# Two transformer layers on one core: small VectorE and GpSimd jobs handed to ScalarE, GpSimd and TensorE

## The chip, the core and the metric

The kernel runs on one core of a Trainium2 chip. The metric is device time in microseconds, the median of several executions; lower is better. A core has TensorE (PE), VectorE (DVE), ScalarE (ACT), GpSimd (POOL) and SyncE (SP), which here only issues DMAs. Each engine works through its own list of instructions in order, and waits on semaphores for the others.

## The reference

The input x is 16 sequences of 256 tokens and 128 numbers. Two parts follow one another, each with a residual and a layer norm behind it:

```python
x = _layernorm(x + _L0_attn_ref(x, ...))      # gated convolution, then 16-head attention in chunks
x = _layernorm(x + _L0_ffn_ref(x, ...))       # two layers of the kind below
def _layer(x, wqkv, qs, ksc, wo, lg, lb, w1, b1, w2, b2):
    h = shift_token(x)                         # half of the columns come from the token before
    q, k, v = split(h @ wqkv)                  # 8 heads of 64
    q, k = l2norm(q) * qs, l2norm(k) * ksc     # l2norm divides by max(norm, 1e-12)
    q, k = rotary_xpos(q, k)
    o = local_attention(q, k, v)               # windows of 64 queries, 128 keys, softmax
    x = x + o @ wo
    h = layernorm(shift_token(x)) * lg + lb
    a, g = split(h @ w1 + b1)                  # 341 + 341 columns
    return x + (a * gelu(g)) @ w2 + b2
```

All is float32. The change touches only the two layers of the second part.

## The kernel before

The kernel has two stages. Stage A does the first part for all 16 sequences; it is not touched. The second stage ("the layers") takes 16 sequences through layer 0 and then layer 1, so 32 units of work. A unit has two tiles of 128 tokens, and each engine's list runs in steps of one tile: an even step (tile 0) and an odd step (tile 1), 64 in all. A loop iteration holds four steps (two units). Nothing is scheduled by a program: the order in which the work of several units is interleaved is written out by hand in each engine's `body`.

A step works on several units at once. For the unit at hand it does the scores, the softmax and the values. For the next unit it prepares q, k and v. For units before it does what follows attention, with lags counted in steps in `F_LATE` ("stats" 4, "norm" 5, "residual" 5, "mT" and "gates" 6, "values" and "down" 7, "yo" 8, "z" 9). So a job with an even lag is done in even steps, and one with an odd lag in odd steps.

The names that matter, by engine, in the order of a step:

- TensorE: the scores (L1420 the mask, L1427 q times k); in an even step the transpose `mT` of the normed hidden state; q or k of the next unit (L1354); the transposes of the softmax weights (L1440); the output product (L1465); q or k again (L1354); a transpose of normalised q or k (L1359); weights times values (L1454); another L1359; v (L1354); in even steps the hidden products (L1372), in odd steps the last product `down` (L1392), which waits for `uT`.
- VectorE: maximum of the scores `fmx` (L1182) and their difference from it (L1186); even steps `hT2 = mT * ln_g + ln_b` (`scaled`, L1085) and `yo` (L1115), odd steps `uT` (L1092) and the layer norm `hc` (`normalised`, L1077, two instructions); the rotation of q or k (L1052, L1053) and its sum of squares (L1055); `mid` (L1146); the sum of the exponentials `f_sum` (L1165) and its reciprocal `f_rsum` (L1168); in odd steps the other two `uT`; the second rotation; and the guard of the norms (`guard`, L1063), which is max(norm squared, 1e-24) on 128x16.
- GpSimd: the multiplication of q or k by the inverse norms (`normalise`, L662, a pair); the sum of the rotated halves (`sums`, L646); the division of the softmax weights by their sums, that is 128x1024 times a broadcast `f_rsum` (L720); in even steps `mrstd` (L688, L690); `sums` again; the inverse norms by a power of -1/2 (`inverse_norms`, L654); in odd steps the residual (`residual`, L698, which adds the second bias b2 to `mid`, and for layer 1 also L704, which adds the residual of stage A).
- ScalarE: squares (L811), copies out of the matmul banks (L873, L832, L886, L823), the exponentials (L878), and in even steps three gelus (L858). A change from exponentials to gelus and back loads a table.

Of the kernel before, what the change touches and what calls it, by code (L numbers as in the profile page):

```python
# [169 lines left out]
def build(nc, t):  # L170

    ctx = ExitStack()
    with ctx:
# [73 lines left out]
        def in_queries(p, at):  # L247
# [34 lines left out]
        resb = [sb(f"resb{p}", [P, 2, TILES, DIM]) for p in range(PAIR)]  # L282
# [150 lines left out]
        def layer_weights(l):  # L433
# [4 lines left out]
            yield b2[l][:, :], t["b2"][l].partition_broadcast(P)  # L438
# [152 lines left out]
        def _(pool):  # L591
            pool.memset(ones[:, :], 1.0).then_inc(consts_set, 1)
            pool.memset(halves[:, :], -0.5).then_inc(consts_set, 1)
            pool.memset(eps[:, :], LN_EPS).then_inc(consts_set, 1)
# [974 lines left out]
```

## Time and profile before

| | |
|---|---|
| median of 3 runs | 1438.56 us (1438.05 to 1438.8) |
| the profiled execution: its own time | 1443.03 us |
| its span, first to last instruction | 1441.2 us |
| stage A | from the start to about 700 us |
| the layers | from about 700 us to the end |
| granted TensorE clock, mean | 0.971 of full speed |

The profile is of one execution. Spans of rows are from the start of the span. A row's duration contains the tail of an instruction, so on VectorE the next one begins some 0.08 us before the end of the one before.

### The profile page before, as it was taken

The page shows a single profiled execution, that of the slowest core. Times are in us where ns is not written, and L with a number is a line of the kernel's source. Part 1 is how long each engine was busy: PE and PEld are TensorE (multiplying, and loading weights), DVE is VectorE, ACT ScalarE, POOL GpSimd, SP SyncE. Part 2 cuts the span into 40 slices and gives each one's busy share as a digit, 9 for nine tenths or more (in the row PEclk, how much of TensorE's full clock was granted, in tenths as well). Part 3 has the DMA queues.
Part 4 walks back from the last instruction along what each step waited for, and adds up shares of the span by engine and source line. Part 5 has one row for each costly group of instructions (what it writes and reads, how often), then busy time and mean ns, then how long its engine had stood idle before and what let it go on. Part 6 is the DMA issues. An engine that isn't in the chain of part 4 may idle for free.

```text
span 1441.2 us, 35736 instructions
## 1 busy us (share of the span) xinstructions
PE 1266.9 (88%) x12288; PEld 987.5 (69%) x12288; DVE 1294.1 (90%) x2514; ACT 872.1 (61%) x1468; POOL 951.0 (66%) x753
## 2 busy tenths in 40 slices
PE   5889899989989889988788999999999889999986
PEld 3577677767767767766566777777777767777764
DVE  4899999999999999997798988999899898999975
ACT  3556566565666656554456676676676657666661
POOL 0733443344433444346799899999999999999973
PEclk8899999999999999998899999999999999999998
DMA  5000000000000000000111112111111121212111
GB/s 170 1 10 13 12 5 11 11 11 11 9 11 11 11 7 5 8 9 14 36 44 41 41 41 49 38 39 42 45 45 48 41 50 43 51 40 49 45 30 31
DMA packets 87332, 44.24 MB, mean 31 GB/s; under 512 B 43938, under 2 KB 80460, under 8 KB 87244
## 3 DMA queue, kind: packets, MB, share of 16 engines
q1 hardware_dynamic: 87244, 43.08, 12.0%
q8 instruction: 54, 0.88, 0.3%
q14 instruction: 34, 0.28, 0.1%
HBM read 19.99 MB, written 6.29 MB: 18 GB/s over the span
## 4 chain that ended last, share of the span: by engine, by line
DVE 39%; issue 23%; POOL 19%; PE 15%; SPq 2%; DVEq 1%; ACT 1%; POOLq 1%; DMA 0%; ACTq 0%
DVE sums L973 9%; DVE probs L1005 7%; POOL rnorm L654 5%; DVE mx L999 4%; POOL kT L646 4%; POOL kT L662 4%; POOL probs L720 4%; PE bank L1372 3%; DVE xo L1034 2%; PE bank L1359 2%; PE bank L1454 2%; PE bank L1427 2%; DVE hc L1077 2%; SPq L475 1%; DVE conv L916 1%
## 5 line engine op out<-in xcount | busy, mean ns | idle before, releaser
L622 POOL TENSOR_TENSOR probs<-probs,coef 128x1024 f32<-128x1024 f32 x128 | 239.5, 1901 | 202.3 <-DVE coef L965 202.3
L795 ACT ACTIVATE probs<-probs 128x1024 f32<-128x1024 f32 x128 | 134.8, 1053 | 100.5 <-DVE probs L1005 100.0
L654 POOL TENSOR_TENSOR rnorm<-norm,halves 128x16 f32<-128x16 f32 x64 | 187.4, 2928 | 3.3
L1274 PE MATMUL bank<-ident,probs 128*128 128x128 f32 x1024 | 143.4, 285 | 49.6 <-POOL probs L622 49.6
L999 DVE TENSOR_REDUCE mx<-bank 128x8 f32<-128x512 f32 x256 | 163.8, 681 | 16.5 <-PE bank L1287 15.2
L782 ACT ACTIVATE wT<-bank 128x512 f32<-128x512 f32 x256 | 138.9, 596 | 65.4 <-PE bank L1274 64.4
L646 POOL TENSOR_TENSOR kT<-qT 128x512 f32<-128x512 f32 x128 | 162.9, 1273 | 22.5 <-DVE qT L1053 20.0
L1005 DVE TENSOR_TENSOR probs<-bank,mx 128x512 f32<-128x512 f32 x256 | 163.6, 680 | 0.0
L1274 PEld LDWEIGHTS bank<-ident,probs 128*128 128x128 f32 x1024 | 115.9, 145 | 68.6 <-POOL probs L622 57.5
L1287 PE MATMUL bank<-kT,qT 64*128 64x256 f32 x1024 | 155.7, 425 | 5.4 <-DVE probs L1005 5.4
L811 ACT ACTIVATE qT<-bank 128x512 f32<-128x512 f32 x128 | 75.9, 593 | 134.0 <-PE bank L1354 126.4
L1313 PE MATMUL bank<-wT,v 128*64 128x128 f32 x2048 | 145.8, 286 | 11.4 <-DVE gate L911 5.7
L973 DVE TENSOR_REDUCE sums<-probs 128x16 f32<-128x1024 f32 x128 | 153.2, 1208 | 0.0
L1313 PEld LDWEIGHTS bank<-wT,v 128*64 128x64 f32 x2048 | 114.4, 141 | 50.3 <-issue 22.0
L720 POOL TENSOR_TENSOR probs<-probs,f_rsum 128x1024 f32<-128x1024 f32 x64 | 121.4, 1897 | 36.0 <-DVE f_rsum L1168 36.0
L662 POOL TENSOR_TENSOR kT<-kT,rnorm 128x512 f32<-128x512 f32 x128 | 131.4, 1047 | 2.7
L1182 DVE TENSOR_REDUCE fmx<-bank 128x4 f32<-128x512 f32 x128 | 82.5, 686 | 51.1 <-PE bank L1427 49.9
L1359 PE MATMUL bank<-ident,kT 128*128 128x128 f32 x512 | 82.7, 285 | 46.2 <-POOL kT L662 44.8
L1287 PEld LDWEIGHTS bank<-kT,qT 64*128 64x128 f32 x1024 | 93.8, 198 | 36.4 <-issue 22.6
L1359 PEld LDWEIGHTS bank<-ident,kT 128*128 128x128 f32 x512 | 57.2, 143 | 77.8 <-POOL kT L662 40.4
L633 POOL TENSOR_TENSOR rstd<-mv,eps 128x1 f32<-128x1 f32 x32 | 6.2, 192 | 157.3 <-DVE mv L1028 157.3
L1372 PE MATMUL bank<-hT,w 128*128 128x256 f32 (+1 forms) x384 | 96.9, 388 | 11.4 <-DVE mid L1146 9.3
(118 smaller groups left out, 3074.2 us busy)
## 6 DMA issues: line engine op xcount, KB each, us to landing
probs<-f_v SPq DMA_DIRECT2D x96, 128.0 KB, 2.3
res<-stage_x SPq DMA_DIRECT2D x48, 128.0 KB, 3.7
xn<-in_x SPq DMA_DIRECT2D x16, 128.0 KB, 2.2
xr<-in_x SPq DMA_DIRECT2D x16, 128.0 KB, 2.1
stage_x<-xo SPq DMA_DIRECT2D x32, 64.0 KB, 1.6
hn<-stage_x SPq DMA_DIRECT2D x32, 64.0 KB
mn<-mid SPq DMA_DIRECT2D x64, 32.0 KB
stage_x<-yo SPq DMA_DIRECT2D x16, 128.0 KB, 2.1
```

The costliest lines, as they stand in the source:

```text
L622: nc.gpsimd.tensor_tensor(out=e[:, :, :, :], in0=e[:, :, :, :], in1=coef[r][:, 2, A_REP * ng:A_REP * (ng + 1), :].unsqueeze(3).broadcast_t ...
L646: nc.gpsimd.tensor_tensor(out=qk[m][:, :, :], in0=on_self[m % 2][:, :, :], in1=on_partner[m % 2][:, :, :], op=ALU.add).then_inc(added, 1)
L654: nc.gpsimd.tensor_tensor(out=rnorm[:, at], in0=norm2[:, 1, at], in1=halves[:, 0:2 * F_HEADS], op=ALU.pow).then_inc(rnorm_set, 1)
L662: nc.gpsimd.tensor_tensor(out=qk[m][:, :, :], in0=qk[m][:, :, :], in1=rnorm[:, F_HEADS * m:F_HEADS * (m + 1)].unsqueeze(2).broadcast_to([P ...
L720: nc.gpsimd.tensor_tensor(out=e, in0=e, in1=f_rsum[s % 2][:, :, :].unsqueeze(3).broadcast_to([P, 2, 4, F_KEYS]), op=ALU.mult).then_inc(f_n ...
L973: nc.vector.tensor_reduce(sums[at % 2][:, A_REP * gg:A_REP * (gg + 1), :], E[(s - SUM_LAG) % E_RING][:, :, :, :], AX.X, ALU.add).then_inc( ...
L999: ins = nc.vector.tensor_reduce(m[:, 2 * k:2 * k + 2, :], both[k][:, :].rearrange("p (h c k) -> p h c k", h=2, c=CHUNKS), AX.X, ALU.max)
L1005: ins = nc.vector.tensor_tensor(e[:, 2 * k:2 * k + 2, :, :], both[k][:, :].rearrange("p (h c k) -> p h c k", h=2, c=CHUNKS), m[:, 2 * k:2 ...
L1274: ins = nc.tensor.transpose(banks[4 + hp][:, P * (2 * kb + hh):P * (2 * kb + hh + 1)], e[:, 2 * hh + hp, 2 * kb:2 * kb + 2, :], ident[:, :])
L1287: ins = nc.tensor.matmul(banks[2 * (s % 2) + h % 2][:, SEQ * (h // 2):SEQ * (h // 2 + 1)], qT[p][lo:lo + A_HD, 2 * g + h // 2, P * tile:P ...
L1313: ins = nc.tensor.matmul(bank[A_HD * hh:A_HD * (hh + 1), P * hp:P * (hp + 1)], v[ap][:, kb, A_HD * og:A_HD * (og + 1)], wT[hp][:, kb, hh, ...
L1359: ins = nc.tensor.transpose(bank[:, P * block_of:P * (block_of + 1)], flat[:, P * block_of:P * (block_of + 1)], ident[:, :])
```

## The change

Five jobs of the layers go to another engine, and the arithmetic stays the same.

1. The division of the softmax weights: GpSimd divides five of eight heads (128x640 instead of 128x1024), and ScalarE the other three, with three copies of 128x128 that are scaled by a column of `f_rsum` (`divided`). TensorE's transposes of the weights wait for both.
2. The guard of the norms goes from VectorE to GpSimd, into `inverse_norms` ahead of the power.
3. The second bias b2 becomes row 85 of the last piece of w2, and row 85 of that piece of `uT` is set to 1 once, at the start. So the last matmul of `down` has 86 rows instead of 85, and no add of b2 is left.
4. The residual: in layer 0 it is now a copy of `mid` on ScalarE (`kept`); in layer 1 it is one add on GpSimd (`mid` and `res1`) where there were two.
5. `hT2 = mT * ln_g + ln_b` goes from VectorE to ScalarE (`hidden_input`), at the start of an even step.

```diff
+F_NORM_ACT = 3
+NORM_FLOOR = 1e-24
@@ weights
-            yield b2[l][:, :], t["b2"][l].partition_broadcast(P)
+            yield w2[l][F_ROWS[-1]:F_ROWS[-1] + 1, F_CHUNKS - 1, :], t["b2"][l:l + 1, :]
@@ gpsimd, start
+            for p in range(PAIR):
+                pool.memset(uT[p][:, F_CHUNKS - 1, :], 1.0).then_inc(consts_set, 1)
@@ gpsimd, inverse_norms
+                    pool.wait_ge(consts_set, N_CONSTS)
+                    pool.wait_ge(norm_step, 4 * unit + 2 * tile + 2)
+                    nc.gpsimd.tensor_scalar_max(norm2[:, 1, at], norm2[:, 0, at], NORM_FLOOR).then_inc(guarded, 1)
                     pool.wait_ge(guarded, TILES * unit + tile + 1)
@@ gpsimd, residual
-                    nc.gpsimd.tensor_tensor(out=resb[p][:, 0, :, :], in0=mid[p][:, :, :],
-                                            in1=b2[layer][:, :].unsqueeze(1).broadcast_to([P, TILES, DIM]),
-                                            op=ALU.add).then_inc(mid_read, 1)
-                    if layer == LAYERS - 1:
-                        pool.wait_ge(res1_in[p], 16 * (it + local // PAIR + 1 - TURNS * layer))
-                        pool.wait_ge(mid_read, unit + 1)
-                        nc.gpsimd.tensor_tensor(out=resb[p][:, 1, :, :], in0=resb[p][:, 0, :, :], in1=res1[p][:, :, :],
-                                                op=ALU.add).then_inc(resb_set, 1)
+                    pool.wait_ge(res1_in[p], 16 * (it + local // PAIR + 1 - TURNS * layer))
+                    nc.gpsimd.tensor_tensor(out=resb[p][:, :, :], in0=mid[p][:, :, :], in1=res1[p][:, :, :],
+                                            op=ALU.add).then_inc(resb_set, 1)
@@ gpsimd, body (residual is called for layer 1 alone)
-                            e = fE[s % F_RING]
+                            e = fE[s % F_RING].rearrange("p k a n -> p (k a) n")[:, 0:F_HEADS - F_NORM_ACT, :]
+                            inverse = f_rsum[s % 2][:, :, :].rearrange("p k a -> p (k a)")[:, 0:F_HEADS - F_NORM_ACT]
                             pool.wait_ge(f_rsum_set, n + 1)
@@ scalar
+                def hidden_input(it, local, layer):
+                    unit = PAIR * it + local
+                    act.wait_ge(f_made["mT"], unit + 1)
+                    nc.scalar.activation(hT2[local % PAIR][:, :], f_bank("mT", local, "middle")[:, 0:SEQ], ACT.Identity,
+                                         bias=ln_b[layer][:, 0:1], scale=ln_g[layer][:, 0:1]).then_inc(f_read["mT"], 1)
+                def kept(it, local):
+                    p, unit = local % PAIR, PAIR * it + local
+                    act.wait_ge(f_read["out"], TILES * unit + TILES)
+                    wait(act, f_read["down"], unit - 1)
+                    nc.scalar.activation(resb[p][:, :, :], mid[p][:, :, :], ACT.Copy).then_inc(mid_kept, 1)
+                def divided(n, s):
+                    e = fE[s % F_RING]
+                    act.wait_ge(f_rsum_set, n + 1)
+                    for a in range(4 - F_NORM_ACT, 4):
+                        ins = nc.scalar.activation(e[:, 1, a, :], e[:, 1, a, :], ACT.Copy, scale=f_rsum[s % 2][:, 1, a:a + 1])
+                    ins.then_inc(f_divided, 1)
@@ scalar, body, behind values_read
+                        if f_exists(turn, s):
+                            divided(n, s)
+                        local = f_late(turn, s, "residual")
+                        if local is not None and layer_of(local) < LAYERS - 1:
+                            kept(it, local)
@@ vector
-                def guard(index, unit, tile):
-                def scaled(it, local, layer):
@@ tensor
+                                rows += c == F_CHUNKS - 1
                     pe.wait_ge(f_normed, late + 1)
+                    pe.wait_ge(f_divided, late + 1)
```

GpSimd, from the division of an odd step in layer 0 to the second `sums` of the even step behind it. Before:

```order
L720 TENSOR_TENSOR probs<-probs,f_rsum 128x1024
L646 TENSOR_TENSOR kT<-qT 128x512
L654 TENSOR_TENSOR rnorm<-norm,halves 128x16
L698 TENSOR_TENSOR resb<-mid,b_0 128x256
L662 TENSOR_TENSOR kT<-kT,rnorm 128x512 x2
L646 TENSOR_TENSOR kT<-qT 128x512
L720 TENSOR_TENSOR probs<-probs,f_rsum 128x1024
L688 TENSOR_TENSOR mrstd<-mmv,eps 128x2
L690 TENSOR_TENSOR mrstd<-mrstd,halves 128x2
L646 TENSOR_TENSOR kT<-qT 128x512
```

The same place in the changed kernel:

```order
L721 TENSOR_TENSOR probs<-probs,f_rsum 128x640
L649 TENSOR_TENSOR kT<-qT 128x512
L657 TENSOR_SCALAR norm<-norm 128x16
L660 TENSOR_TENSOR rnorm<-norm,halves 128x16
L668 TENSOR_TENSOR kT<-kT,rnorm 128x512 x2
L649 TENSOR_TENSOR kT<-qT 128x512
L721 TENSOR_TENSOR probs<-probs,f_rsum 128x640
L694 TENSOR_TENSOR mrstd<-mmv,eps 128x2
L696 TENSOR_TENSOR mrstd<-mrstd,halves 128x2
L649 TENSOR_TENSOR kT<-qT 128x512
```

The division is smaller, a guard stands ahead of each power, and nothing stands any more between the power of an odd step and the pair of multiplications that opens the even step.

ScalarE, from the copy of v in an even step to the second half of the next odd step's weights (wq holds the transposed weights). Before:

```order
L823 ACTIVATE f_v<-bank 128x512
L858 ACT_TABLE_LOAD
L858 ACTIVATE ge<-bank,b_0 128x256 x2
L858 ACTIVATE ge<-bank,b_0 85x256
L816 ACTIVATE fhT_high<-bank 128x256
L811 ACTIVATE qT<-bank 128x512
L873 ACTIVATE wq<-bank 128x512 x2
L878 ACT_TABLE_LOAD
L878 ACTIVATE probs<-probs 128x1024
```

The same place in the changed kernel:

```order
L824 ACTIVATE f_v<-bank 128x512
L881 ACTIVATE probs<-probs,f_rsum 128x128 x3
L859 ACT_TABLE_LOAD
L859 ACTIVATE ge<-bank,b_0 128x256 x2
L859 ACTIVATE ge<-bank,b_0 85x256
L817 ACTIVATE fhT_high<-bank 128x256
L812 ACTIVATE qT<-bank 128x512
L899 ACTIVATE wq<-bank 128x512 x2
L904 ACT_TABLE_LOAD
L904 ACTIVATE probs<-probs 128x1024
```

The three scaled copies stand ahead of the gelus, and so also ahead of the next step's exponentials; the number of table loads is the same.

## Rows read from the trace of the kernel before

**Rows 1.** The page: busy time, share of the span, instructions of each engine.

```profile
PE 1266.9 (88%) x12288; PEld 987.5 (69%) x12288; DVE 1294.1 (90%) x2514; ACT 872.1 (61%) x1468; POOL 951.0 (66%) x753
```

**Rows 2.** Busy time by stretch: PE, PEld, DVE, ACT, POOL, clock, DMA share, GB/s.

```profile
900.00:1000.00 100.00, 93.39 (x1019) 72.84 (x1018) 91.34 (x180) 66.37 (x106) 90.33 (x67) 1.00 0.17 39
1250.00:1350.00 100.00, 89.69 (x983) 70.33 (x976) 91.42 (x202) 64.57 (x104) 94.97 (x78) 1.00 0.19 46
```

**Rows 3.** Timeline, VectorE, one unit in layer 0: start, duration, line, count, idle before.

```profile
907.83 0.68 DVE L1053 TENSOR_TENSOR qT<-bank,table 128x512 f32<-128x512 f32 x1
...
910.51 1.29 DVE L1182 TENSOR_REDUCE fmx<-bank 128x4 f32<-128x512 f32 x2 [0.62 <-PE bank L1427]
...
912.91 0.54 DVE L1085 TENSOR_SCALAR hT<-bank,ln_g,ln_b 128x256 f32<-128x256 f32 x1
...
916.92 0.20 DVE L1168 RECIPROCAL f_rsum<-f_sum 128x8 f32<-128x8 f32 x1
...
920.91 1.29 DVE L1182 TENSOR_REDUCE fmx<-bank 128x4 f32<-128x512 f32 x2 [0.84 <-PE bank L1427]
...
924.04 1.32 DVE L1077 TENSOR_SCALAR hc<-mn,mmv,mrstd 128x128 f32<-128x128 f32 x2
...
927.27 1.20 DVE L1165 TENSOR_REDUCE f_sum<-probs 128x8 f32<-128x1024 f32 x1
...
932.73 1.29 DVE L1182 TENSOR_REDUCE fmx<-bank 128x4 f32<-128x512 f32 x2 [0.62 <-PE bank L1427]
```

**Rows 4.** Timeline, GpSimd, the same unit.

```profile
908.59 1.27 POOL L646 TENSOR_TENSOR kT<-qT 128x512 f32<-128x512 f32 x1
909.97 2.90 POOL L654 TENSOR_TENSOR rnorm<-norm,halves 128x16 f32<-128x16 f32 x1
912.83 0.73 POOL L698 TENSOR_TENSOR resb<-mid,b 128x256 f32<-128x256 f32 x1
913.52 2.05 POOL L662 TENSOR_TENSOR kT<-kT,rnorm 128x512 f32<-128x512 f32 x2
...
917.21 1.90 POOL L720 TENSOR_TENSOR probs<-probs,f_rsum 128x1024 f32<-128x1024 f32 x1 [0.41 <-DVE f_rsum L1168]
919.06 0.19 POOL L688 TENSOR_TENSOR mrstd<-mmv,eps 128x2 f32<-128x2 f32 x1
...
924.22 2.06 POOL L662 TENSOR_TENSOR kT<-kT,rnorm 128x512 f32<-128x512 f32 x2
```

**Rows 5.** Timeline, ScalarE, the same unit.

```profile
918.39 1.28 ACT L858 ACT_TABLE_LOAD   x1
...
924.84 1.06 ACT L878 ACTIVATE probs<-probs 128x1024 f32<-128x1024 f32 x1
```

**Rows 6.** Timeline, GpSimd and VectorE, the first odd step with `hc` beside loaded lists.

```profile
767.96 2.05 POOL L662 TENSOR_TENSOR kT<-kT,rnorm 128x512 f32<-128x512 f32 x2
...
768.28 1.81 DVE L1077 TENSOR_SCALAR hc<-mn,mmv,mrstd 128x128 f32<-128x128 f32 x2
```

**Rows 7.** Timeline, GpSimd, one unit in layer 1.

```profile
1281.05 1.90 POOL L720 TENSOR_TENSOR probs<-probs,f_rsum 128x1024 f32<-128x1024 f32 x1 [0.51 <-DVE f_rsum L1168]
...
1288.11 2.15 POOL L662 TENSOR_TENSOR kT<-kT,rnorm 128x512 f32<-128x512 f32 x2
...
1298.67 0.72 POOL L698 TENSOR_TENSOR resb<-mid,b 128x256 f32<-128x256 f32 x1
...
1300.24 2.04 POOL L662 TENSOR_TENSOR kT<-kT,rnorm 128x512 f32<-128x512 f32 x2
...
1304.03 1.90 POOL L720 TENSOR_TENSOR probs<-probs,f_rsum 128x1024 f32<-128x1024 f32 x1 [0.51 <-DVE f_rsum L1168]
```

**Rows 8.** Timeline, VectorE, the same unit in layer 1.

```profile
1287.77 0.59 DVE L1077 TENSOR_SCALAR hc<-mn,mmv,mrstd 128x128 f32<-128x128 f32 x2
...
1296.31 1.29 DVE L1182 TENSOR_REDUCE fmx<-bank 128x4 f32<-128x512 f32 x2
```

**Rows 9.** Costliest groups, whole run: busy us, mean ns, idle before.

```profile
L816 ACT ACTIVATE fhT_high<-bank 128x256 fp32r<-128x256 f32 x32 | 12.3, 385 | 13.5 <-PE bank L1346 13.5
```

More of the change, by code:

```diff
@@ L281, in build @@
         res1 = [sb(f"res1_{p}", [P, TILES, DIM]) for p in range(PAIR)]
-        resb = [sb(f"resb{p}", [P, 2, TILES, DIM]) for p in range(PAIR)]
+        resb = [sb(f"resb{p}", [P, TILES, DIM]) for p in range(PAIR)]
         yo = [sb(f"yo{p}", [P, TILES, DIM]) for p in range(PAIR)]
@@ L728, in body @@
                         local = f_late(turn, s, "residual")
-                        if local is not None:
-                            residual(it, local, layer_of(local))
+                        if local is not None and layer_of(local) == LAYERS - 1:
+                            residual(it, local, LAYERS - 1)
                 both_layers(pool, body, pre)
@@ L1039, in layers_program, with rotate @@
             def layers_program():
-                def rotate(index, local, m, turn, layer):
+                def rotate(index, before, local, m, turn, layer):
                     tile, kind = divmod(m, 2)
@@ L1079, in normalised @@
                     ins.then_inc(hc_set, 1)
-                def scaled(it, local, layer):
-                    unit = PAIR * it + local
-                    dve.wait_ge(f_made["mT"], unit + 1)
-                    nc.vector.tensor_scalar(hT2[local % PAIR][:, :], f_bank("mT", local, "middle")[:, 0:SEQ], ln_g[layer][:, 0:1],
-                                            ln_b[layer][:, 0:1], ALU.mult, ALU.add).then_inc(f_read["mT"], 1)
                 def gated_product(c, bank, col, par, unit, layer):
@@ L1112, in finished @@
                     dve.wait_ge(f_made["down"], unit + 1)
[L1113 removed]
+                    dve.wait_ge(resb_set if last_layer else mid_kept, b + 1)
                     wait(dve, m_out[par], 16 * (it + turn_of))
                     nc.vector.tensor_tensor(yo[par][:, :, :], f_bank("down", local, "middle")[:, 0:TILES * DIM].rearrange("p (t d) -> p t d", t=TILES),
[L1116 removed]
+                                            resb[par][:, :, :], ALU.add).then_inc(f_read["down"], 1)
                     if last_layer:
@@ L1143, in attended @@
                     dve.wait_ge(res_in[local % PAIR], 16 * (it + local // PAIR + 1))
-                    wait(dve, mid_read, unit - 1)
+                    if layer_of(local - PAIR) == LAYERS - 1:
+                        wait(dve, resb_set, unit - 1 - BATCH * (LAYERS - 1))
+                    else:
+                        wait(dve, mid_kept, unit - 1)
                     wait(dve, mn_in[local % PAIR], 80 * (it + local // PAIR))
@@ L1167, in exponentials_summed @@
                     wait(dve, f_normed, n - 1)
+                    wait(dve, f_divided, n - 1)
                     nc.vector.reciprocal(f_rsum[s % 2][:, :, :], f_sum[s % 2][:, :, :]).then_inc(f_rsum_set, 1)
@@ L1213, in body @@
                             at = 2 * tile + 1
-                            rotate(4 * (unit + 1) + at, 4 * (p + 1) + at, at, turn, layer_of(p + 1))
-                            guard(4 * (unit + 1) + at, unit + 1, tile)
+                            rotate(4 * (unit + 1) + at, unit, 4 * (p + 1) + at, at, turn, layer_of(p + 1))
                         if late("z") is not None and layer_of(late("z")) == LAYERS - 1:
```

38 lines of the change are left out of this document (15 added, 23 removed).

## The prediction

> **What bounds the kernel now.** I first read the busy shares [rows 1]. Over the whole span VectorE is at 90% and GpSimd at 66%, but GpSimd's share is an average of two stages. So I read the stretches of the layers [rows 2]: there GpSimd is at 90% in layer 0 and 95% in layer 1, VectorE at 91% in both, TensorE at 93% and 90%, ScalarE at 65%. Nobody is full; three engines hand work round in a ring and each waits a little. So no busy sum gives the time, and I followed the ring through one unit in the timeline.
>
> In layer 0 the even step's first maximum starts at 910.51 and the next unit's at 932.73 [rows 3]: a unit takes 22.22 us. The reader should see four links in it, of which I use the starts:
>
> - 910.51 to 917.21, 6.70 us: VectorE works from the maximum to `f_rsum` without a wait (it ends at 916.92 + 0.20), then GpSimd, which waited 0.41 us for it, starts the division [rows 3, 4].
> - 917.21 to 924.22, 7.01 us: GpSimd without a wait: division, `mrstd`, sum, power, up to the next step's pair of multiplications L662 [rows 4].
> - 924.22 to 925.36, 1.14 us: VectorE's pair `hc` starts at 924.04, and ends 1.32 us later [rows 3]. The same pair takes 0.59 us in layer 1, at 1287.77 [rows 8], where GpSimd's pair starts 0.34 us later than it [rows 7]. Here it starts 0.18 us later, and `hc` ends 0.1 us after the first of the two multiplications (2.06 / 2, so 925.25) [rows 4]. In an earlier unit L662 began first, at 767.96; `hc` came at 768.28, took 1.81 us and ended at 770.09, that is 0.08 us after the end of both multiplications [rows 6]. So one `hc` instruction that meets a running multiplication waits for its end. How many of the two are caught depends on a few tenths: none at a lead of 0.34 us, one at 0.18, both at a lag.
> - 925.36 to 932.73, 7.37 us: VectorE to `uT`, the last product on TensorE and the next scores [rows 3].
>
> 6.70 + 7.01 + 1.14 + 7.37 = 22.22: this ring sets layer 0. The Trainium skill, SBUF — State Buffer, section "Who interferes with whom", gives the reason: VectorE's two-port instructions and GpSimd's share a port pair as an exclusive lock, and whichever starts first makes the other wait for its whole instruction. The three cases above agree. Were the pair shared by bandwidth instead, `hc` would take about 0.6 us wherever it falls, the unit of layer 0 in the sum below would be 6.25 + 6.67 + 0.19 + 0.59 + 7.37 = 21.07 instead of 22.42, and the change would gain some 17 us there instead of losing 3.
>
> In layer 1 the unit is 1281.05 to 1304.03, 22.98 us [rows 7]. Its links are 7.72 (maximum at 1296.31 to division at 1304.03 [rows 7, 8]), 7.06 (1281.05 to 1288.11), and 8.20 from that pair to the next maximum (1288.11 to 1296.31), through TensorE alone, since `hc` is free there: 22.98.
>
> **The change, priced.**
>
> *Division.* GpSimd's broadcast multiplication takes 1.90 us for 1024 columns and 2.05 / 2 = 1.03 for 512 [rows 4]; on the line between them 640 columns take 1.25. That is -0.64 us (1.90 - 1.25, rounded) on the second link.
>
> *Guard on GpSimd.* A GpSimd instruction of this kind isn't in the trace. Below, the add of 128x2 takes 0.19 us [rows 4]; above, the power of the same 128x16 takes 2.90 [rows 4]. It is a plain elementwise operation like the first, and 14 more columns at the broadcast multiplication's 1.7 ns each (0.87 us for 512 columns) add 0.02; with a wait on its own result I take 0.30, between the two ends. On the second link: +0.30. On VectorE the guard's going saves a few tenths at the end of steps, where VectorE then waits for TensorE (0.62 and 0.84 us [rows 3]), so nothing.
>
> *`hT2` to ScalarE.* It takes 0.54 us on VectorE, of which 0.45 is start to start (the overlap is 0.08), in the first link [rows 3]: -0.45. On ScalarE 256 columns take 0.385 [rows 9] in a gap at the start of the even step.
>
> *Residual.* It lies between GpSimd's power and the pair of the even step: 912.83 to 913.52, in layer 1 1298.67 to 1300.24 [rows 4, 7]. It isn't in the ring above, but moves the pair of the even step, by which TensorE's scores and so `hc` are timed. Without it in layer 0 that pair could start 0.08 us behind the power's end at 912.87, so 0.57 earlier; in layer 1 one add is left, 1.57 - 0.73 = 0.84 earlier. The guard delays it: from the sum's start at 908.59 to the power's at 909.97 are 1.38 us now [rows 4], and will be 1.23 (the sum) + 0.30: +0.15. The shorter division gives nothing here, since that sum waits for the rotation, 907.83 + 0.68 = 908.51 [rows 3, 4].
>
> *ScalarE.* Three copies of 128 columns, each at least half of 0.385 us and at most all of it [rows 9], so 0.6 to 1.15 us a step; I take 0.8. In an even step they stand ahead of a table load that now starts as soon as it can, at 918.39, and push back all behind it. The next exponentials start at 924.84 and end at 925.90, and the sum that reads them starts at 927.27 [rows 3, 5]: 1.37 us of cover. So nothing; without the cover each tenth over it would cost a tenth per unit. The wait of TensorE for `f_divided` is covered by more than 2 us (the transposes come in the next step).
>
> *`down` with 86 rows, the two memsets, one DMA less broadcast:* nothing; the columns stream as before, and the start waits for DMAs.
>
> **Sum for layer 0.** New links: 6.70 - 0.45 = 6.25; 7.01 - 0.64 + 0.30 = 6.67. Where does `hc` fall? From the maximum, L662 starts at 6.25 + 6.67 = 12.92. `hc` starts behind three pieces: the even pair at 913.52 - 910.51 = 3.01, less 0.57, plus 0.15, so 2.59; to the odd maximum 7.39 (913.52 to 920.91); to `hc` 3.13 (920.91 to 924.04) [rows 3, 4]. Together 13.11, so it now lags by 0.19 us where it led by 0.18. Both of the pair are caught, as at 768.28, and it ends 2.13 us (770.09 - 767.96) after the start of L662 instead of 1.14. The unit: 6.25 + 6.67 + 2.13 + 7.37 = 22.42, that is 0.20 slower than now.
>
> **Sum for layer 1.** 7.72 - 0.45 = 7.27; 7.06 - 0.34 = 6.72; L662 at 13.99. `hc`: 3.93 (1296.31 to 1300.24) - 0.84 + 0.15 = 3.24, + 7.39 + 3.13 = 13.76. It leads by 0.23 us (now 0.34): one is caught. Then 7.27 + 6.72 + 1.14 + 7.37 = 22.50, against 22.98: -0.48. Through TensorE it would be 7.27 + 6.72 + 8.20 = 22.19, which no longer binds.
>
> **All.** The pattern of layer 0 holds from the fourth unit until the residual of layer 1 begins, some 15.5 units; that of layer 1 for some 11.6. 15.5 x 0.20 = +3.1; 11.6 x -0.48 = -5.6. In the first three units GpSimd has fewer jobs around it and, I estimate, its saving of 2 x 0.34 counts whole: -2. The last units and the tail: an estimate of -1.5 from one shorter division and less waiting. Sum -6.0. The profiled execution took 1443.03 us, 4.5 over the median; so 1437.0 for such a one and 1432.6 for the median.
>
> **The rivals.**
>
> - *The lag isn't reached in layer 0* (my phases are off by 0.3 us). One of `hc` is caught as now, and the other chain binds, through the even pair: it is 0.42 us earlier (0.57 - 0.15), 22.22 - 0.42 = 21.80. 15.5 x -0.42 = -6.5 instead of +3.1: 1423. For it: the phase is a difference of long chains. Against: it must err by 0.3 in one direction. 16%.
> - *In layer 1 none is caught* (a lead over 0.3): 22.19 a unit, -9.2 instead of -5.6: 1429. 10%.
> - *The other side: the guard on GpSimd costs more.* It is once on the ring of each of 27 units, so each 0.1 us costs 2.7 us. From 0.30 + 6.0 / 27 = 0.52 on, the change is no gain. At 0.7 it is +4.8: 1443. The far end, the power's 2.90 and a wait, would give 1432.6 + 27 x 2.7, about 1505; against it speaks that a power is no plain operation, and that the plain one of few columns takes 0.19 [rows 4]. 13%.
> - *Both are caught in layer 1* (a lead under 0.1): 23.5 a unit, +5.9 instead of -5.6: 1444. 10%.
> - *ScalarE becomes late* (copies with a scale from a column at over 1.37 us for three, or its waits): each step's exponentials hold VectorE. At 2 us, 0.6 x 32 = +19, less 6: 1452. 5%.
>
> The main forecast keeps 46%. **What follows.** A measurement of this kernel can tell about 0.2%, 2.9 us, from no change. Faster: 39 of the main case's 46 and both first rivals, 65%. Same: 12%. Slower: 23%. The range takes in the first rival and both of the slower ones near 1443: 1420 to 1443.
>
> **What would show it.** Right: L721 at 1.25 us, L657 near 0.2, units of 22.4 us in layer 0 with an `hc` pair of about 2 us, and of 22.5 in layer 1 with a pair of about 1.3. Waits of VectorE for the scores grow beyond 0.6 and 0.8 us. Wrong: `hc` pairs of 1.3 in layer 0; a guard over 0.5 us; `f_sum` waiting for ScalarE.

## The result, and the profile after

| | us, median (lowest to highest) |
|---|---|
| before, measured with it | 1438.68 (1438.05 to 1440.41), 4 runs |
| after | 1430.21 (1429.87 to 1431.28), 4 runs |
| ratio | 0.9939, 95% interval 0.9926 to 0.9951 |

The change makes the kernel 8.5 us faster. The profiled execution took 1430.35 us, with a span of 1428.5. The first part of the page of the kernel after, with the columns of [rows 1]:

```profile
PE 1258.4 (88%) x12288; PEld 984.8 (69%) x12288; DVE 1262.2 (88%) x2418; ACT 943.0 (66%) x1708; POOL 905.3 (63%) x787
```

Two stretches of it, for [rows 2] (length, busy time of each engine with the number of instructions, granted clock, DMA share, GB/s):

```profile
900.00:1000.00 100.00, 90.73 (x1001) 71.76 (x998) 86.77 (x164) 74.70 (x142) 82.11 (x70) 1.00 0.17 40
...
1250.00:1350.00 100.00, 91.77 (x1013) 72.33 (x1013) 90.53 (x194) 78.48 (x142) 91.25 (x87) 1.00 0.19 45
```

GpSimd fell from 90 to 82 in layer 0, and VectorE from 91 to 87. Yet layer 0 became slower, as the starts of the first maxima show. The timeline of VectorE after, for [rows 3] (start, duration, engine, line, operation, tiles, shapes, count, idle time before it and what ended it):

```profile
907.18 1.29 DVE L1202 TENSOR_REDUCE fmx<-bank 128x4 f32<-128x512 f32 x2 [1.41 <-PE bank L1445]
...
913.14 0.20 DVE L1188 RECIPROCAL f_rsum<-f_sum 128x8 f32<-128x8 f32 x1
...
917.32 1.29 DVE L1202 TENSOR_REDUCE fmx<-bank 128x4 f32<-128x512 f32 x2 [1.33 <-PE bank L1445]
...
920.44 1.94 DVE L1102 TENSOR_SCALAR hc<-mn,mmv,mrstd 128x128 f32<-128x128 f32 x2
...
929.75 1.29 DVE L1202 TENSOR_REDUCE fmx<-bank 128x4 f32<-128x512 f32 x2 [1.40 <-PE bank L1445]
```

And GpSimd in the same unit, for [rows 4]:

```profile
906.49 0.26 POOL L657 TENSOR_SCALAR norm<-norm 128x16 f32<-128x16 f32 x1
906.83 2.93 POOL L660 TENSOR_TENSOR rnorm<-norm,halves 128x16 f32<-128x16 f32 x1
909.93 2.04 POOL L668 TENSOR_TENSOR kT<-kT,rnorm 128x512 f32<-128x512 f32 x2 [0.17 <-POOL rnorm L660]
...
913.42 1.26 POOL L721 TENSOR_TENSOR probs<-probs,f_rsum 128x640 f32<-128x640 f32 x1 [0.21 <-DVE f_rsum L1188]
...
915.59 1.27 POOL L649 TENSOR_TENSOR kT<-qT 128x512 f32<-128x512 f32 x1
916.83 0.25 POOL L657 TENSOR_SCALAR norm<-norm 128x16 f32<-128x16 f32 x1
917.24 2.93 POOL L660 TENSOR_TENSOR rnorm<-norm,halves 128x16 f32<-128x16 f32 x1 [0.16 <-POOL norm L657]
920.25 2.05 POOL L668 TENSOR_TENSOR kT<-kT,rnorm 128x512 f32<-128x512 f32 x2
```

The unit is 907.18 to 929.75, 22.57 us (22.48 to 22.49 in every other one), against 22.22 before. Its links are 6.24 (907.18 to 913.42), 6.83 (to 920.25), 2.13 (to 922.38, the end of `hc`) and 7.37. The pair `hc` starts 0.19 us behind the pair of multiplications, takes 1.94 us, and ends 0.08 after both of them.

ScalarE around the table load, for [rows 5]:

```profile
914.67 0.97 ACT L881 ACTIVATE probs<-probs,f_rsum 128x128 f32<-128x128 f32 x3
915.66 1.28 ACT L859 ACT_TABLE_LOAD   x1
...
921.24 1.06 ACT L904 ACTIVATE probs<-probs 128x1024 f32<-128x1024 f32 x1
```

Layer 1 is where the time came back. GpSimd, for [rows 7]:

```profile
1224.83 2.04 POOL L668 TENSOR_TENSOR kT<-kT,rnorm 128x512 f32<-128x512 f32 x2
...
1228.85 1.25 POOL L721 TENSOR_TENSOR probs<-probs,f_rsum 128x640 f32<-128x640 f32 x1 [0.74 <-DVE f_rsum L1188]
...
1232.25 0.26 POOL L657 TENSOR_SCALAR norm<-norm 128x16 f32<-128x16 f32 x1
1232.67 3.04 POOL L660 TENSOR_TENSOR rnorm<-norm,halves 128x16 f32<-128x16 f32 x1 [0.16 <-POOL norm L657]
1235.80 2.04 POOL L668 TENSOR_TENSOR kT<-kT,rnorm 128x512 f32<-128x512 f32 x2
```

VectorE, for [rows 8]:

```profile
1221.58 1.29 DVE L1202 TENSOR_REDUCE fmx<-bank 128x4 f32<-128x512 f32 x2 [0.31 <-PE bank L1445]
...
1235.34 0.59 DVE L1102 TENSOR_SCALAR hc<-mn,mmv,mrstd 128x128 f32<-128x128 f32 x2
...
1239.82 0.88 DVE L1110 SCALAR_TENSOR_TENSOR uT<-bank,b,ge 128x256 f32<-128x256 f32 x2 [0.54 <-PE bank L1389]
...
1243.89 1.29 DVE L1202 TENSOR_REDUCE fmx<-bank 128x4 f32<-128x512 f32 x2 [0.31 <-PE bank L1445]
```

The unit is 22.31 us (22.98 before): 7.27 + 6.95 + 8.09. `hc` leads the multiplications by 0.46 us and takes 0.59, so nobody holds it up. It holds up GpSimd instead: the power that ends beside it takes 3.04 us here, and 3.13 in the next unit, where 2.93 is its usual length:

```profile
1254.90 3.13 POOL L660 TENSOR_TENSOR rnorm<-norm,halves 128x16 f32<-128x16 f32 x1
```

The last link goes through TensorE, for which VectorE waits before `uT` and before the maximum.

The two spans differ by 12.7 us, and the starts of the first maxima divide that up: the 15 units of layer 0 in its steady pattern took 337.65 us where they had taken 333.02 (+4.6); three units in which the layers overlap 67.2 for 70.9 (-3.7); nine units of layer 1 200.6 for 206.7 (-6.1); the first four units 78.1 for 80.4 (-2.3); the tail 50.95 for 53.15 (-2.2); and -3.1 lies ahead of the first unit. That last part is a difference between two executions: in the profiles of this document the point lies anywhere between 692.1 and 697.1 us, with and without the two memsets of the change (and the profiled execution of before was 4.5 us over its median). Of the -3.7, 2.1 us come from a single unit of the kernel before, 24.43 us long, in which both of `hc` were caught although it led by 0.08:

```profile
1171.79 2.20 DVE L1077 TENSOR_SCALAR hc<-mn,mmv,mrstd 128x128 f32<-128x128 f32 x2
```

### The profile page after: what moved, and what is told of

Same layout as the page of the kernel before. It is cut to its first block, busy times and chain, and to the rows that moved or that the text cites. A ratio compares the mean times of both kernels' runs of the same rounds, so it can differ in the third digit from the quotient of the medians.

```text
span 1428.5 us, 36014 instructions
## 1 busy us (share of the span) xinstructions
PE 1258.4 (88%) x12288; PEld 984.8 (69%) x12288; DVE 1262.2 (88%) x2418; ACT 943.0 (66%) x1708; POOL 905.3 (63%) x787
## 4 chain that ended last, share of the span: by engine, by line
DVE 45%; issue 19%; POOL 17%; PE 16%; DVEq 1%; ACT 1%; POOLq 0%; DMA 0%; SPq 0%; ACTq 0%
DVE sums L1004 9%; DVE probs L1036 7%; POOL rnorm L660 7%; DVE mx L1030 5%; POOL kT L668 4%; PE bank L1389 3%; POOL kT L649 3%; DVE xo L1065 2%; DVE hc L1102 2%; DVE qT L1084 2%; PE bank L1376 2%; PE bank L1473 2%; PE bank L1445 2%; DVE f_sum L1184 2%; DVE conv L947 1%
## 5 line engine op out<-in xcount | busy, mean ns | idle before, releaser
L649 POOL TENSOR_TENSOR kT<-qT 128x512 f32<-128x512 f32 x128 | 162.7, 1272 | 53.8 <-DVE qT L1084 53.6
L660 POOL TENSOR_TENSOR rnorm<-norm,halves 128x16 f32<-128x16 f32 x64 | 188.9, 2952 | 6.1 <-POOL norm L657 1.5
L668 POOL TENSOR_TENSOR kT<-kT,rnorm 128x512 f32<-128x512 f32 x128 | 131.1, 1045 | 4.3 <-POOL rnorm L660 0.7
L1304 PEld LDWEIGHTS bank<-kT,qT 64*128 64x128 f32 x1024 | 94.9, 200 | 37.1 <-issue 23.6
L721 POOL TENSOR_TENSOR probs<-probs,f_rsum 128x640 f32<-128x640 f32 x64 | 80.4, 1256 | 37.4 <-DVE f_rsum L1188 37.4
L1371 PE MATMUL bank<-wqkv_high,fhT_high 128*128 128x512 f32 x192 | 93.8, 489 | 3.9 <-DVE fhT_low L1152 1.0
```

The source lines that it names most:

```text
L649: nc.gpsimd.tensor_tensor(out=qk[m][:, :, :], in0=on_self[m % 2][:, :, :], in1=on_partner[m % 2][:, :, :], op=ALU.add).then_inc(added, 1)
L660: nc.gpsimd.tensor_tensor(out=rnorm[:, at], in0=norm2[:, 1, at], in1=halves[:, 0:2 * F_HEADS], op=ALU.pow).then_inc(rnorm_set, 1)
L668: nc.gpsimd.tensor_tensor(out=qk[m][:, :, :], in0=qk[m][:, :, :], in1=rnorm[:, F_HEADS * m:F_HEADS * (m + 1)].unsqueeze(2).broadcast_to([P ...
L1304: ins = nc.tensor.matmul(banks[2 * (s % 2) + h % 2][:, SEQ * (h // 2):SEQ * (h // 2 + 1)], qT[p][lo:lo + A_HD, 2 * g + h // 2, P * tile:P ...
```

## The experiments

Each was measured with the kernel before on the same chip, which is not the same for all experiments; units and pairs are of the profiled execution; "unit" is the distance of the first maxima of successive even steps in the steady pattern. Ratios are to the kernel before as measured beside each, at medians of 1439.1 to 1440.3 us.

| | us | ratio (95%) | unit, layer 0 | layer 1 | `hc` pair |
|---|---|---|---|---|---|
| before | 1438.7 | | 22.2 | 23.0 | 1.3; 0.6 |
| after | 1430.2 | 0.9939 (0.9926 to 0.9951) | 22.5 | 22.3 | 1.9; 0.6 |
| 1 after, `hc` first | 1410.5 | 0.9789 (0.9774 to 0.9804) | 21.2 | 22.2 | 0.6 |
| 2 before, `hc` first | 1430.2 | 0.9933 (0.9919 to 0.9947) | 21.8 | 22.8 | 0.6 |
| 3 guards in even steps | 1426.1 | 0.9909 (0.9894 to 0.9924) | 22.0 or 21.8 | 22.6 | 1.4 or 0.6 |
| 4 guards in odd steps | 1448.7 | 1.0065 (1.0049 to 1.0080) | 22.6 | 23.6 | 1.6; 2.0 |
| 5 after, no division by ScalarE | 1428.4 | 0.9927 (0.9912 to 0.9942) | 21.8 | 22.8 | 0.6 |
| 6 division alone | 1450.4 | 1.0077 (1.0064 to 1.0090) | 22.8 | 23.8 | 1.9; 2.0 |
| 7 as 1, four heads | 1414.4 | 0.9828 (0.9808 to 0.9848) | 21.2 | 22.1 | 0.6 |
| 8 as 1, three more copies | 1412.7 | 0.9807 (0.9790 to 0.9823) | 21.3 | 22.2 | 0.6 |
| 9 `hc` at the even step's end | 1406.5 | 0.9775 (0.9762 to 0.9789) | 21.1 | 22.2 | 1.3 to 1.4 |
| 10 residual alone | 1436.9 | 0.9978 (0.9968 to 0.9988) | 21.8 | 22.8 | 0.6 |
| 11 hidden input alone | 1456.1 | 1.0115 (1.0100 to 1.0131) | 22.8 | 23.8 | 1.9 |
| 12 as 1, no division by ScalarE | 1428.7 | 0.9923 (0.9909 to 0.9936) | 21.8 | 22.8 | 0.6 |

**1 and 2. `hc` ahead of the two jobs before it in the odd step.** Only the order changes: the same instructions, VectorE's pair 0.7 us earlier.

```diff
                             ins.then_inc(f_sub, 1)
+                        if late("norm") is not None:
+                            normalised(late("norm") % PAIR, PAIR * it + late("norm"))
                         if tile == 1 and prepares(turn, p, 2):
                             low_part(it, p + 2, turn)
                         if late("values") is not None:
                             mixed(it, late("values"), layer_of(late("values")))
-                        if late("norm") is not None:
-                            normalised(late("norm") % PAIR, PAIR * it + late("norm"))
```

> The changed kernel, with hc (the pair of VectorE instructions of the layer norm) moved ahead of fhT_low and the first uT in the odd step, so it starts some 0.7 us earlier and leads GpSimd's pair by about 0.5 us. Port theory (hc caught by both multiplications costs the ring 1 to 1.4 us a unit in layer 0): hc pairs of 0.59 us in layer 0, units of 21.1 to 21.8 us there instead of 22.5, layer 1 unchanged at 22.3; total 11 to 21 us below the changed kernel, so about 1410 to 1420. Rival (layer 0 is held by ScalarE's added work or by TensorE's wait for its copies, and the long hc lies in slack): hc pairs short, units still 22.5, total within 3 us of 1430.

> The kernel before, with the same move of hc. Port theory: the 0.73 us that one caught instruction costs go from the ring; the second chain of the prediction (22.22 less 0.73, so 21.5) or GpSimd binds, units of 21.5 to 21.9 in layer 0, layer 1 unchanged at 23.0: 5 to 11 us below before, about 1430, so as fast as the whole change. Rival: within 3 us of before.

With the change (experiment 1), VectorE:

```profile
901.44 1.29 DVE L1202 TENSOR_REDUCE fmx<-bank 128x4 f32<-128x512 f32 x2 [1.41 <-PE bank L1445]
...
913.98 0.59 DVE L1102 TENSOR_SCALAR hc<-mn,mmv,mrstd 128x128 f32<-128x128 f32 x2
```

and GpSimd in the same unit:

```profile
914.52 2.05 POOL L668 TENSOR_TENSOR kT<-kT,rnorm 128x512 f32<-128x512 f32 x2
```

`hc` leads by 0.54 us and takes 0.59, so its second instruction has begun when the multiplications start at 914.52. Layer 0 falls by 1.3 us a unit and the kernel by 20; layer 1, where `hc` was already free, stays. Experiment 2 takes the single catch out of the kernel before: 22.2 to 21.8. So the kernel before lost some 9 us to this meeting of two instructions, and the change made it lose 20.

**3 and 4. More work for GpSimd.** Two guards whose result nobody reads stand ahead of the real one, in the even steps (3) or in the odd ones (4).

```diff
                     pool.wait_ge(norm_step, 4 * unit + 2 * tile + 2)
+                    if tile == 0:                # experiment 4: tile == 1
+                        for k in range(2):
+                            nc.gpsimd.tensor_scalar_max(spare[:, tile, k, :], norm2[:, 0, at], NORM_FLOOR)
```

> The changed kernel, with two more guards on GpSimd in even steps only (written to a spare tile, 0.25 us each), ahead of the real one. They delay the pair of the odd step by 0.5 us, so that hc, now 0.17 us late, leads by 0.33. Port theory: hc is caught once or not at all in layer 0, units of 21.7 to 22.0 instead of 22.5; in layer 1, where nothing is caught now, 22.6 to 22.8 instead of 22.3. Total 2 to 8 us below the changed kernel, although GpSimd does more. Rival (GpSimd's work on the ring simply adds): +0.5 us for each of 27 units, 13 us above the changed kernel.

> The changed kernel, with the two more guards in odd steps only. They delay the pair of the even step, and with it the scores that time hc. Port theory: layer 0 stays at 22.5 to 22.8 (both are caught already), layer 1 goes from a lead of 0.46 to none, both caught, 23.4 to 23.7 instead of 22.3; total 13 to 19 us above the changed kernel, nearly all of it in layer 1. Rival (simply adds): +0.5 in both layers.

Experiment 3, the spare work on GpSimd, its multiplications, and `hc` on VectorE with the maxima around it:

```profile
916.63 0.46 POOL L660 TENSOR_SCALAR spare<-norm 128x16 f32<-128x16 f32 x2
...
920.47 2.05 POOL L672 TENSOR_TENSOR kT<-kT,rnorm 128x512 f32<-128x512 f32 x2
```

```profile
906.98 1.29 DVE L1206 TENSOR_REDUCE fmx<-bank 128x4 f32<-128x512 f32 x2 [1.41 <-PE bank L1449]
...
920.25 1.35 DVE L1106 TENSOR_SCALAR hc<-mn,mmv,mrstd 128x128 f32<-128x128 f32 x2
...
928.97 1.29 DVE L1206 TENSOR_REDUCE fmx<-bank 128x4 f32<-128x512 f32 x2 [1.41 <-PE bank L1449]
```

The spare guards add 0.46 us to the ring and make the kernel 4 us faster than without them: `hc` now leads by 0.22, one of the pair is caught instead of both, and this unit takes 21.99. In 9 of the 15 steady units of layer 0 none is caught, and they take some 21.75. The same work in the odd steps delays `hc` instead (through the even pair and TensorE's scores), and in layer 1, where it had been free, both are caught: some 18 us slower than the change. No account by busy time alone gives these two signs.

**5, 6 and 12. The division.** In 5 and 12 the changed kernel divides all eight heads on GpSimd again; 12 has `hc` first as well. Experiment 6 is the kernel before with the division's part alone.

```diff
-F_NORM_ACT = 3
+F_NORM_ACT = 0
@@ scalar, body
-                        if f_exists(turn, s):
-                            divided(n, s)
@@ vector and tensor
-                            wait(dve, f_divided, n - 1)
-                    pe.wait_ge(f_divided, late + 1)
```

> The changed kernel with its first part undone: GpSimd divides all eight heads again, ScalarE none. That puts 0.64 us back on the second link. Port theory: the pair of the odd step starts 0.64 us later, at 13.64 after the even maximum, so hc at 13.17 leads by 0.47 and is free; then the way through TensorE binds (8.13 us from the pair to the next maximum, as with the two more guards in even steps): units of 21.8 in layer 0 instead of 22.5, and of 22.8 in layer 1 instead of 22.3. Total 3 to 6 us BELOW the changed kernel, although GpSimd has 0.64 us more in each of 64 steps. Rival (the division was a gain of its own, as the work taken off a full engine): 0.64 us for each of 27 units, 17 us above the changed kernel.

> The kernel before, with the first part of the change alone: three heads divided on ScalarE. Port theory: the odd pair starts at 13.72 - 0.64 = 13.08 in layer 0 while hc stays at 13.53, so both are caught and hc ends at 15.2: a unit of 22.6 instead of 22.2. In layer 1 the pair comes at 14.15 and hc at 14.44, both caught, 23.6 instead of 23.0. Total 10 to 14 us ABOVE before, about 1451. Rival: -0.64 us a unit, 17 us below before.

> hc first, with the division undone (GpSimd divides all eight heads). hc is free with and without the division, so the division now shows its own worth: units of 21.8 and 22.8, as with hc late and all eight heads, against 21.2 and 22.2. Total 14 to 19 us ABOVE hc first, about 1427; without hc first the same part cost 2 to 5 us.

Experiment 6, `hc` between the maxima, and below it GpSimd's pair:

```profile
904.76 1.29 DVE L1195 TENSOR_REDUCE fmx<-bank 128x4 f32<-128x512 f32 x2 [0.62 <-PE bank L1440]
...
918.28 1.94 DVE L1089 TENSOR_SCALAR hc<-mn,mmv,mrstd 128x128 f32<-128x128 f32 x2
...
927.59 1.29 DVE L1195 TENSOR_REDUCE fmx<-bank 128x4 f32<-128x512 f32 x2 [0.62 <-PE bank L1440]
```

```profile
918.06 2.07 POOL L663 TENSOR_TENSOR kT<-kT,rnorm 128x512 f32<-128x512 f32 x2
```

The guard, which VectorE still does in this kernel, in the same unit:

```profile
914.14 0.78 DVE L1075 TENSOR_SCALAR norm<-norm 128x16 f32<-128x16 f32 x1
```

Alone, the part that takes most work off GpSimd costs about 11 us: the division is 0.64 us shorter, the multiplications come 0.41 earlier (0.49 in every other unit), and `hc`, which had led by 0.18, lags by 0.22 (0.31). The rest of the 0.64 goes to a second meeting that my list lacked: the guard is a VectorE instruction that can be caught too. It takes 0.17 us where it is free, here 0.78, until GpSimd's sum beside it is over, and the power then waits 0.19 us for it. In the changed kernel the removal of the division costs nothing that can be measured (1428.4 against 1430.2, intervals overlap; 3 to 6 us below were expected): layer 0 gains 0.7 a unit by a free `hc` and layer 1 loses 0.5, and its profile has one unit of 24.42 us with a fall of the granted clock. But where `hc` is out of the way it is worth 18 us (12 against 1): one and the same edit, +11, 0 or -18.

**7. Four heads on ScalarE, 8. three more copies.** Both with `hc` first.

```diff
-F_NORM_ACT = 3
+F_NORM_ACT = 4
@@ experiment 8, ahead of the dividing copies
+                    for k in range(3):
+                        nc.scalar.activation(spare[:, s % 2, k, :], ident, ACT.Copy, scale=f_rsum[s % 2][:, 1, k:k + 1])
```

> hc first, and four heads on ScalarE instead of three: GpSimd's division at 128x512 takes 1.05 us instead of 1.26, ScalarE has one copy more (0.32 us). In layer 0 TensorE and VectorE now close the ring without GpSimd's division, so units stay at 21.2; in layer 1 the division is still on the ring, 22.0 instead of 22.2. Total 1 to 4 us below hc first with three heads.

> hc first, and three more copies of 128x128 on ScalarE in each step, to a spare tile, ahead of the three that divide; they add about 0.95 us to ScalarE's step. Its cover in the odd step with hc first is 0.64 us (the exponentials end at 916.57, the sum that reads them starts at 917.21). If ScalarE has become the next bound, units grow by 0.3 to 0.7 us in layer 0 and by 0 to 0.4 in layer 1, 5 to 14 us in all, and f_sum waits for the exponentials. If ScalarE is still covered, nothing.

A fourth head came 4 us above experiment 1 where 1 to 4 below were expected. Its steady units are as short as or 0.1 shorter than those of experiment 1. But the shorter division brings the multiplications forward once more: `hc` leads by 0.33 to 0.55 in layer 0, mostly less than the 0.54 of experiment 1, and in three units it is caught. They start at 748.64 (a pair of 2.05 us, unit 24.45 against 22.44 in experiment 1; the granted clock falls there too, to 0.60 from 765 to 769), at 984.99 (1.39, unit 22.00 against 21.2) and at 1091.56 (2.04, unit 23.18 against 22.45). In this profile that is 3.5 us, more than the shorter units give. That the fourth head gains nothing is measured; why its runs scatter from 1410.6 to 1418.8 is open, since only one of the quicker ones was profiled. Three unused copies, 1 us of ScalarE a step, cost 0.1 a unit in layer 0 and nothing in layer 1, 2 us in all: ScalarE is just covered, and is not the bound.

**9. `hc` at the end of the even step**, half a unit earlier, where VectorE waits for the scores.

```diff
-    "norm": 5,
+    "norm": 4,
@@ vector, body: the two lines of `normalised` go from behind `mixed` to here
+                        if late("norm") is not None:
+                            normalised(late("norm") % PAIR, PAIR * it + late("norm"))
                         if late("z") is not None and layer_of(late("z")) == LAYERS - 1:
                             closed(it, late("z"))
```

> The changed kernel with hc moved to the end of the even step before, into the 1.4 us in which VectorE waits there for TensorE's scores. GpSimd's sum runs then, so the first of the pair is caught (pair of about 1 us), but off the ring; and fhT_low, for which TensorE waits 0.6 to 0.8 us a unit with hc first, is early again. Units of 21.0 to 21.2 in layer 0 (21.2 with hc first), 22.2 in layer 1. Total 0 to 4 us below hc first. If a caught instruction cost the ring wherever it stands, layer 0 would stay at 22 or more.

```profile
907.79 1.30 DVE L1102 TENSOR_SCALAR hc<-mn,mmv,mrstd 128x128 f32<-128x128 f32 x2
...
909.22 1.29 DVE L1202 TENSOR_REDUCE fmx<-bank 128x4 f32<-128x512 f32 x2
...
930.29 1.29 DVE L1202 TENSOR_REDUCE fmx<-bank 128x4 f32<-128x512 f32 x2
```

GpSimd beside it:

```profile
907.49 1.27 POOL L649 TENSOR_TENSOR kT<-qT 128x512 f32<-128x512 f32 x1
```

The two maxima shown are those of odd steps, 21.07 us apart. Here GpSimd's sum (L649) catches one of the pair, 1.30 us instead of 0.59, and that costs nothing on the ring: it lies in the wait of some 1.3 us that VectorE has there anyway (as before the maximum at 917.32 in the kernel after), and the maximum has no wait of its own left. This version has the lowest median, 1406.5 us, 24 below the change and 32 below the kernel before; the intervals of its ratio and of that of experiment 1 overlap, so the two can't be told apart.

**10 and 11. The residual (parts 3 and 4), and the hidden input (part 5), each alone** in the kernel before.

```diff
+                            kept(it, local)                           # 10, ScalarE, layer 0
-                            residual(it, local, layer_of(local))      # 10, GpSimd: layer 1 alone, one add
-                            scaled(it, late("gates"), layer_of(late("gates")))      # 11, VectorE
+                            hidden_input(it, local, layer_of(local))                # 11, ScalarE
```

> The kernel before with the third and fourth part alone (b2 as a row of w2, the residual as a copy on ScalarE or one add). The even pair starts 0.57 us earlier and with it the scores that time hc, the odd pair does not: hc leads by 0.75 and is free. The way through TensorE binds: 6.70 + 7.01 + 8.13 = 21.84 in layer 0 instead of 22.2; 22.8 to 23.0 in layer 1. Total 5 to 9 us below before, about 1432, as much as the whole change. Rival (the residual is 0.7 us of GpSimd off the ring and hc has slack): within 3 us of before.

> The kernel before with the fifth part alone: hT2 on ScalarE. The odd pair starts 0.45 us earlier (13.27 in layer 0, 14.33 in layer 1), hc does not (13.53, 14.44): both are caught in both layers. 6.25 + 7.01 + 2.13 + 7.37 = 22.8 in layer 0 instead of 22.2, 7.27 + 7.06 + 2.13 + 7.37 = 23.8 in layer 1 instead of 23.0. Total 14 to 20 us ABOVE before, though VectorE has 0.45 us less in each unit. Rival: 0.45 us a unit below before, 12 us.

Alone, part 5 is the most harmful: 0.45 us off VectorE pulls GpSimd's division and all behind it forward, but not `hc`. In a unit of experiment 11, GpSimd:

```profile
927.61 2.11 POOL L662 TENSOR_TENSOR kT<-kT,rnorm 128x512 f32<-128x512 f32 x2
```

and VectorE:

```profile
927.86 1.94 DVE L1087 TENSOR_SCALAR hc<-mn,mmv,mrstd 128x128 f32<-128x128 f32 x2
```

A lag of 0.25, both caught, +17 us. The residual does the opposite, it brings the even pair and so `hc` forward: 0.4 us less a unit in layer 0, 0.15 in layer 1. That should have given 7 us (15 x 0.38 + 9 x 0.15), and 5 to 9 were expected; the total fell by 2 to 3 only. Part of the rest is in the granted clock (below): three units of layer 1 in its profile take 24.4 us instead of 22.8. A unit of 23.55 ahead of them has another cause, one of `hc` is caught in it (1.31 us).

## Why the prediction was right, and where it was off

Forecast 1432.6 (1420 to 1443), measured 1430.2.

- **The ring and its links.** Right. The links of layer 0 were forecast at 6.25, 6.67, 2.13 and 7.37 and measured at 6.24, 6.83, 2.13 and 7.37. Experiments 1 to 4 show that where `hc` meets the multiplications decides: they move `hc` and nothing else (1 and 2), or add work (3 and 4), and the time follows the meeting.
- **Layer 0: both are caught.** Right: lag 0.19 forecast, 0.19 measured. `hc` at 13.26 from the maximum for 13.11, the pair at 13.07 for 12.92. That the lag came out to the hundredth is luck: two errors of 0.15 moved both alike. On the pair's side it is the guard (0.11) and a power 0.03 longer; on `hc`'s side, through the even pair, mostly a wait of 0.17 us for the power's result at 909.93, for which I had put 0.08. 22.48 to 22.57 for 22.42, so +4.6 us for +3.1.
- **Why an instruction is caught.** By the Trainium skill, SBUF — State Buffer, "Who interferes with whom", the two engines take their port pair as an exclusive lock, not as shared bandwidth, and the first to issue holds it for its whole instruction. The traces agree for the multiplications: `hc` ends 0.08 us after the multiplication it met. They limit it for the power. In experiment 12 `hc` runs wholly inside it, and both take their usual time:

```profile
918.56 2.93 POOL L660 TENSOR_TENSOR rnorm<-norm,halves 128x16 f32<-128x16 f32 x1 [0.16 <-POOL norm L657]
```

```profile
920.39 0.60 DVE L1100 TENSOR_SCALAR hc<-mn,mmv,mrstd 128x128 f32<-128x128 f32 x2
```

  And in layer 1 after the change, where `hc` starts 0.2 to 0.3 us before the power should end, `hc` keeps its 0.59 us and the power, which started first, gets longer. So not every GpSimd instruction holds the pair throughout; the measurement decides.
- **Layer 1: one is caught.** Wrong; this step failed. `hc` came at 13.76, as forecast to the hundredth, but the multiplications at 14.22 instead of 13.99, so the lead was 0.46 instead of 0.23 and none was caught. The forecast let GpSimd's own work alone set the start of the multiplications. The traces show that `hc` sets it too: it makes the power ahead of them 3.04 to 3.14 us long, where the 50 powers of the layers beside which no `hc` runs take 2.93 or 2.94, and they start 0.46 us behind `hc` in seven of the nine steady units. Where the power took 3.13, as at 1254.90, they would have started at 14.02 with a power of 2.93, a lead of 0.26, close to the 0.23 forecast; the other 0.2 is `hc`'s own doing. The leads of 0.34 and 0.46 in layer 1 of the kernel before, from which I took the edge, had been made in the same way (a power of 2.94 to 3.08 instead of 2.90). The edge is narrow. In the changed kernel `hc` starts 2.74 to 2.75 us behind the start of the power in those units and is free; in layer 0 of experiment 3 it is free at 2.76 and 2.77, either at 2.78, and caught at 2.79; in experiment 7 it was caught once at 2.75. The unit is 22.31 through TensorE, near the 22.19 of the rival with 10%, which I had rated too low. The error was in my favour: -6.1 over nine units.
- **The guard.** Mis-sized: 0.25 us itself, and with the wait of 0.16 for its own result 0.42 in even steps, against 0.30. In the unit shown (1232.25) that is half of the 0.23 by which the multiplications came late; the rest is in the power, which `hc` held up (3.13 from L660 to L668 against 3.01 in layer 0). Its table row:

```profile
L657 POOL TENSOR_SCALAR norm<-norm 128x16 f32<-128x16 f32 x64 | 16.1, 252 | 0.1
```

- **The division on GpSimd, 1.25.** Right (1.26 at 913.42), and the copies on ScalarE mis-sized (0.97 for 0.8, at 914.67) without effect, as experiment 8 shows.
- **`hT2` and the even pair.** Right in size (6.24; the even pair at 2.75 for 2.59 in layer 0 and 3.25 for 3.24 in layer 1). VectorE's wait for the scores grew from 0.62 and 0.84 to 1.41 and 1.33, as expected: this is where the work taken off VectorE went in layer 0.
- **The sum.** Layer 0 +4.6 (forecast +3.1), the start of the layers -2.3 (-2), the transition and layer 1 -9.8 (-5.6), the tail -2.2 (-1.5): -9.6 in all beside the 3.1 ahead of the layers. The medians differ by 8.5, the forecast was 6.0. Part of that closeness is luck: layer 0 was 1.5 us worse than forecast and the rest some 5 better, of which 2.1 come from the one unit at the change of layers that the forecast did not look at.

So the change gains less than its parts can. With `hc` free in both kernels it is worth 20 us (1430.2 in experiment 2, 1410.5 in experiment 1). With `hc` in its old place the kernel before loses 9 us to the meeting and the kernel after 20, and of the 20 gained 8.5 are left.

## What to carry to other kernels

When two engines lock each other out instruction by instruction, price an edit by where it moves the meeting, not by the work it removes: list the pairs that can meet (a VectorE instruction that takes longer in one place than in another, as `hc` and the guard do here, shows one), with their leads in tenths of a microsecond, and work out both starts after the edit. An instruction that can be caught belongs in a wait of its own engine or well ahead of its opponent; moving it is worth trying before any work is moved between engines, and a verdict on an edit (+11, 0 or -18 us for the same division here) holds only for the phase in which it was measured. A forecast whose case turns on 0.2 us should spread its chances over both sides of that edge.

## What was not expected of the hardware

How many of a pair are caught follows the lead of its start over the multiplications' start: none at 0.46 (after, layer 1), 0.54 (experiment 1) and 0.34 [rows 7, 8]; one at 0.22 (experiment 3) and 0.18 [rows 3, 4]; both at lags of 0.19 to 0.25. All profiles but that of experiment 9 together: none in 240 pairs at leads of 0.33 and more; one in 30 at 0.08 to 0.26; both in 104 from a lead of 0 to a lag of 0.60. Three fall outside: both at a lead of 0.08 (the unit of 24.43 us in the kernel before), and one at lags of 0.97 and 0.98 (experiment 6). Leads of 0.34 and 0.46 come up so often because `hc` itself lengthens the power ahead of the multiplications.

TensorE's granted clock falls in the middle of a well-filled stage. In experiment 10 three such falls hit layer 1. The maxima on either side of one unit:

```profile
1242.43 1.29 DVE L1190 TENSOR_REDUCE fmx<-bank 128x4 f32<-128x512 f32 x2
...
1266.86 1.29 DVE L1190 TENSOR_REDUCE fmx<-bank 128x4 f32<-128x512 f32 x2
```

and stretches of that unit, with the columns of [rows 2]:

```profile
1256.00:1258.00 2.00, 0.87 (x3) 0.38 (x3) 2.00 (x6) 1.99 (x3) 1.92 (x2) 1.00 0.00 0
...
1258.00:1260.00 2.00, 1.71 (x28) 1.54 (x30) 1.97 (x4) 0.93 (x2) 1.92 (x4) 0.79 0.04 8
...
1260.00:1262.00 2.00, 2.00 (x17) 1.65 (x14) 0.10 (x1) 0.60 (x1) 2.00 (x3) 0.50 0.26 72
1262.00:1264.00 2.00, 2.00 (x11) 1.38 (x10) 1.21 (x3) 0.75 (x2) 1.25 (x1) 0.86 0.07 18
```

The unit takes 24.4 us instead of 22.8. From 1258 to 1264 the clock lost 0.42 + 1.00 + 0.28 = 1.70 us, what 3.4 us at the lower level, 1.2 GHz, would cost. It fell after TensorE had waited 1.42 us for GpSimd's multiplications (L663); VectorE then stands still. A stretch of the unit before it in the same profile:

```profile
1234.00:1236.00 2.00, 0.57 (x4) 0.42 (x4) 2.00 (x5) 1.50 (x2) 1.92 (x3) 1.00 0.00 0
```

There TensorE is as idle and its clock does not fall, so the wait alone does not decide it. What does stays open. All eleven runs of experiment 10 have a mean granted clock of 0.967 to 0.970, the runs of the kernel before beside them 0.969 to 0.978, and the profiles of experiments 5 and 12 have one unit of 24.42 us each, at 0.93.
